# Causal masks of a first score pass: from accumulating matmuls in PSUM to VectorE's add-and-minimum instruction

## The reference

```python
x = x + 0.5 * ffn(layernorm(x))      # 8 experts, I = 512, silu(x G^T) * (x U^T) D^T, top-p routing
x = x + attn(layernorm(x))           # 16 query heads of 16, 4 key/value heads, RMS norm, rope
x = x + 0.5 * ffn(layernorm(x))
# inside attn
attn = jnp.einsum('bhqd,bhkd->bhqk', q * scale, k)
attn = jnp.where(causal[None, None], attn, -jnp.inf)
attn = jax.nn.softmax(attn, axis=-1)
```

## Time and profile before

| | |
|---|---|
| median of 3 runs | 1226.78 us (1225.18 to 1227.13) |
| the profiled execution, its own time | 1226.45 us |
| its span in the profile | 1224.7 us |
| busy PE, DVE, POOL, ACT | 95%, 65%, 55%, 47% |

### The profile page before, as it was taken

The page is one execution under the profiler, slowest core; times in us unless marked ns, Lnnn a source line. Parts: engine busy times, 40 slices in busy tenths (PEclk is TensorE's granted clock), DMA queues, the critical chain, the costliest instruction groups (busy, mean ns, idle before and its releaser), DMA issues.

```text
span 1224.7 us, 22657 instructions
## 1 busy us (share of the span) xinstructions
PE 1165.3 (95%) x8315; PEld 701.2 (57%) x8315; DVE 796.2 (65%) x1571; ACT 578.0 (47%) x954; POOL 669.8 (55%) x740
## 2 busy tenths in 40 slices
PE   4699999998999899999899999899999999999998
PEld 2355555565555566666566566566565565666655
DVE  5688787567866766666766667767567555554444
ACT  3444454343456545555455554554644545333332
POOL 4454334357567766666666677577564546333332
PEclk9799999999999999999999999999999999999999
DMA  6112120000000000000000000000000000000000
GB/s 217 45 56 82 52 65 1 1 1 1 1 1 1 1 1 2 1 1 2 1 2 1 1 1 2 1 18 2 1 2 1 18 1 1 1 10 9 1 1 19
DMA packets 10107, 19.25 MB, mean 16 GB/s; under 512 B 2192, under 2 KB 6800, under 8 KB 10000
## 3 DMA queue, kind: packets, MB, share of 16 engines
q1 hardware_dynamic: 8992, 14.64, 3.7%
q10 hardware_dynamic: 1008, 3.15, 0.7%
HBM read 15.70 MB, written 2.10 MB: 15 GB/s over the span
## 4 chain that ended last, share of the span: by engine, by line
PE 69%; DVE 7%; POOL 3%; issue 2%; ACT 1%; DVEq 0%; ACTq 0%; POOLq 0%
PE YB L297 20%; PE G L278 19%; PE U L278 19%; PE S L420 2%; POOL RR L1067 1%; PE S L446 1%; PE S L461 1%; DVE TS L680 1%; PE S L352 1%; DVE MXN L891 1%; DVE TS L684 1%; ACT TS L509 1%; PE S L392 1%; PE S L396 1%; PE S L398 1%
## 5 line engine op out<-in xcount | busy, mean ns | idle before, releaser
L1011 POOL TENSOR_TENSOR HS<-TS,HS 128x512 f16<-128x512 f32 x256 | 303.1, 1184 | 433.5 <-ACT HS L516 433.1
L680 DVE SCALAR_TENSOR_TENSOR TS<-TS,G 128x512 f32<-128x512 f32 x256 | 175.6, 686 | 372.0 <-ACT TS L509 371.6
L297 PE MATMUL YB<-W,HS 128*128 128x256 f16 x3036 | 374.7, 273 | 20.3 <-DVE X L700 20.3
L278 PE MATMUL G<-XS,W 128*128 128x512 f16 x1536 | 377.5, 382 | 2.9 <-ACT W L523 1.8
L278 PE MATMUL U<-XS,W 128*128 128x512 f16 x1536 | 376.4, 381 | 0.0
L297 PEld LDWEIGHTS YB<-W,HS 128*128 128x128 f16 x3036 | 292.2, 98 | 98.7 <-DVE X L700 29.9
L509 ACT ACTIVATE TS<-G,TSC 128x512 f32<-128x512 f32 x256 | 175.5, 686 | 297.5 <-PE U L278 290.9
L516 ACT ACTIVATE HS<-TS 128x512 f16<-128x512 f32 x256 | 161.2, 630 | 273.8 <-DVE TS L684 268.1
L278 PEld LDWEIGHTS U<-XS,W 128*128 128x128 f16 x1536 | 151.1, 98 | 183.9 <-issue 4.4
L278 PEld LDWEIGHTS G<-XS,W 128*128 128x128 f16 x1536 | 147.6, 98 | 136.4 <-issue 6.4
L684 DVE SCALAR_TENSOR_TENSOR TS<-TS,U 128x512 f32<-128x512 f32 x256 | 175.8, 687 | 8.8
(11 more groups left out here) (160 smaller groups left out, 861.6 us busy)
## 6 DMA issues: line engine op xcount, KB each, us to landing
out_y<-X SPq DMA_DIRECT2D x16, 128.0 KB, 1.7
X<-in_x SPq DMA_DIRECT2D x3, 512.0 KB, 6.1
room<-in_gate SPq DMA_DIRECT2D x3, 512.0 KB, 3.1
room<-in_up SPq DMA_DIRECT2D x3, 512.0 KB, 3.2
room<-in_down SPq DMA_DIRECT2D x3, 512.0 KB, 3.9
QKT<-in_gate SPq DMA_DIRECT2D x3, 512.0 KB, 3.6
QKT<-in_up SPq DMA_DIRECT2D x3, 512.0 KB, 3.7
QKT<-in_down SPq DMA_DIRECT2D x3, 512.0 KB, 4.5
```

The source lines that it names most:

```text
L278: mm = eng.matmul(bank[:, :], W[:, e, wl, jj, kk * I + m * P:kk * I + (m + 1) * P], flat(XS16[:, b % 2, xl, kk, :, :], 'cq'), start=q == 0 ...
L297: mm = eng.matmul(out, HS[:, j % 2, hl, kk, m * P:(m + 1) * P], W[:, e, wl, 2, kk * D:(kk + 1) * D], start=kk + hl + wl == 0, stop=kk == K ...
L680: eng.scalar_tensor_tensor(TS[:, k % 3, :], TS[:, k % 3, :], 1.0, GB[k % 2][:, :], ALU.add, ALU.mult).then_inc(L['v_t'].sem, 1)
L1011: eng.tensor_tensor(HS[:, j % 2, 1, m, :], TS[:, k % 3, :], HS[:, j % 2, 0, m, :], ALU.subtract).then_inc(L['g_lo'].sem, 1)
```

## The change

`pe_max` leaves the mask matmuls out and signals after the last score matmul of each bank. MB becomes two blocks of 128 columns, the first all 0, the second the mask. `dve_max` no longer reduces a bank in one instruction: for each head it issues one `tensor_tensor_reduce`, which computes (scores + mask) x -1, writes it back over the scores in PSUM, and gives the minimum of it. That is 8 instructions of 128 columns in an even pass and 4 of 256 columns in an odd one, instead of 2 of 512 columns. RWR, a small tile used before the first routing, now lies in LG, and `flat` is defined earlier.

```diff
-        RWR = sb('RWR', [P, 2, KD, E], F32)
+        RWR = LG[:, :, :].rearrange('p (a k) e -> p a k e', a=2)
-        MB = sb('MB', [P, P], F16)
+        MB = sb('MB', [P, 2, P], F16)
...
-                        eng.matmul(bank[:, q * P:(q + 1) * P], QT1[rows(h), 2 * kv + q % 2, :], keys[rows(h), 0, kv, :], start=q == 0, stop=False, skip_group_check=True, tile_position=(64 * h, 0))
-                for bank in (S0, S1):
-                    mm = eng.matmul(bank[:, :].rearrange('p (g k) -> p g k', g=G), ident16[:, :], MB[:, :].unsqueeze(1).broadcast_to([P, G, P]), start=False, stop=True, skip_group_check=True)
+                        mm = eng.matmul(bank[:, q * P:(q + 1) * P], QT1[rows(h), 2 * kv + q % 2, :], keys[rows(h), 0, kv, :], start=q == 0, stop=q == 3, skip_group_check=True, tile_position=(64 * h, 0))
+                        if q == 3:
+                            mm.then_inc(L['p_mx'].sem, 1)
...
-                for bank in (S0, S1):
-                    mm = eng.matmul(bank[:, :].rearrange('p (a b) -> p a b', a=2)[:, :, P:2 * P], ident16[:, :], MB[:, :].unsqueeze(1).broadcast_to([P, 2, P]), start=False, stop=True, skip_group_check=True)
-            mm.then_inc(L['p_mx'].sem, 1)
...
+            if n == 0:
+                eng.wait_ge(s_i2, 2)
+            heads, width = (4, P) if t % 2 == 0 else (2, 2 * P)
+            mask = flat(MB[:, :, :], 'ak')[:, 2 * P - width:]
             for h, bank in ((0, S0), (1, S1)):
-                if t % 2 == 0:
-                    x, out = (bank[:, :].rearrange('p (a g k) -> p a g k', a=2, g=2), MXN[:, 2 * j:2 * j + 2, :, h])
-                else:
-                    x, out = (bank[:, :].rearrange('p (g k) -> p g k', g=2), MXN[:, j, :, h])
-                eng.tensor_reduce(out, x, AX.X, ALU.max, negate=True).then_inc(L['v_mp'].sem, 1)
+                for g in range(heads):
+                    out = MXN[:, 2 * j + g // 2, g % 2, h:h + 1] if t % 2 == 0 else MXN[:, j, g, h:h + 1]
+                    x = bank[:, g * width:(g + 1) * width]
+                    mx = eng.tensor_tensor_reduce(x, x, mask, -1.0, 3.0e38, ALU.add, ALU.min, out)
+                mx.then_inc(L['v_mp'].sem, 1)
```

More of the change, by code:

```diff
@@ L115, in sem, with flat @@
             return ctx.enter_context(nc.semaphore(name))
+        def flat(ap, dims):
+            return ap.rearrange(f"p {' '.join(dims)} -> p ({' '.join(dims)})")
         X = sb('X', [P, NT, D], F32)
@@ L395, in pe_max @@
                     for h, bank in ((0, S0), (1, S1)):
-                        eng.matmul(bank[:, q * 2 * P:(q + 1) * 2 * P], QT1[rows(h), 2 * j + q, :], keys[rows(h), :, j, :], start=q == 0, stop=False, skip_group_check=True, tile_position=(64 * h, 0))
-                for bank in (S0, S1):
-                    mm = eng.matmul(bank[:, :].rearrange('p (a b) -> p a b', a=2)[:, :, P:2 * P], ident16[:, :], MB[:, :].unsqueeze(1).broadcast_to([P, 2, P]), start=False, stop=True, skip_group_check=True)
-            mm.then_inc(L['p_mx'].sem, 1)
+                        mm = eng.matmul(bank[:, q * 2 * P:(q + 1) * 2 * P], QT1[rows(h), 2 * j + q, :], keys[rows(h), :, j, :], start=q == 0, stop=q == 1, skip_group_check=True, tile_position=(64 * h, 0))
+                        if q == 1:
+                            mm.then_inc(L['p_mx'].sem, 1)
         def pe_qtp2(eng, t, s):
@@ L555, in act_qc @@
             if t:
-                eng.wait_ge(*L['p_mx'].at(MAXN[t - 1], 'ab'))
+                eng.wait_ge(*L['p_mx'].at(MAXN[t - 1], 'b'))
             eng.wait_ge(*L['p_qt'].at(t, 'q'))
@@ L882, in dve_max @@
             t, j = MAXP[n]
-            eng.wait_ge(*L['p_mx'].at(n, 'ab'))
+            eng.wait_ge(*L['p_mx'].at(n, 'b'))
             if j == 0:
                 eng.wait_ge(*L['v_mm'].at(t - 1, 'm2'))
+            if n == 0:
+                eng.wait_ge(s_i2, 2)
+            heads, width = (4, P) if t % 2 == 0 else (2, 2 * P)
+            mask = flat(MB[:, :, :], 'ak')[:, 2 * P - width:]
             for h, bank in ((0, S0), (1, S1)):
-                if t % 2 == 0:
-                    x, out = (bank[:, :].rearrange('p (a g k) -> p a g k', a=2, g=2), MXN[:, 2 * j:2 * j + 2, :, h])
-                else:
-                    x, out = (bank[:, :].rearrange('p (g k) -> p g k', g=2), MXN[:, j, :, h])
-                eng.tensor_reduce(out, x, AX.X, ALU.max, negate=True).then_inc(L['v_mp'].sem, 1)
+                for g in range(heads):
[3 more added lines that the diff above has]
+                mx.then_inc(L['v_mp'].sem, 1)
         def dve_mm(eng, t):
@@ L1231, in _ @@
             eng.memset(LOW[:, :, :], 1.0).then_inc(s_i1, 1)
-            eng.memset(MB[:, :], 0.0).then_inc(s_i1, 1)
+            eng.memset(MB[:, :, :], 0.0).then_inc(s_i1, 1)
             eng.wait_ge(s_i1, 7)
             eng.affine_select(out=LOW[:, :, :], in_=LOW[:, :, :], compare_op=ALU.is_ge, fill=0.0, base=-1, pattern=[[1, E], [-1, E]], channel_multiplier=0).then_inc(s_i1, 1)
-            eng.affine_select(out=MB[:, :], in_=MB[:, :], compare_op=ALU.is_ge, fill=MASKED, base=0, pattern=[[-1, P]], channel_multiplier=1).then_inc(s_i2, 1)
+            eng.affine_select(out=MB[:, 1, :], in_=MB[:, 1, :], compare_op=ALU.is_ge, fill=MASKED, base=0, pattern=[[-1, P]], channel_multiplier=1).then_inc(s_i2, 1)
             eng.memset(VS[:, :, :, :, :], 1.0).then_inc(s_i2, 1)
```

2 lines of the change are left out of this document (removed), and 2 rows, old and new, of the table L.

## The result

The changed kernel takes **1229.61 us** (median of 20 runs, 1224.23 to 1233.93), the kernel before 1226.13 (20 runs, 1223.71 to 1227.47); the ratio is **1.0026**, 95% interval 1.0015 to 1.0036. It is slower by about 3.5 us, where I forecast 1.5 us faster. The profiled execution took 1229.79 us, its span is 1228.0 (1224.7 before).

The account below looks back on a forecast made before the run. It took TensorE, busy 95% of the span, to bound the kernel, with VectorE holding it in places. Terms 3.2 - 3.0 - 0.7 - 1.0 = -1.5 us took 1226.78 to 1225.3 us, range 1221.0 to 1232.5.

Parts of the forecast that it names:

- the opening: VectorE's queue is full there, so its longer passes delay L700 and TensorE: 0.99 + 4 x 0.56 = +3.2 us.
- three batches without routing: Masks save 1.57 us before a last pass without slack, which loses 0.56: -1.01 each, -3.0 us.
- three with routing: Two odd passes on the VectorE and GpSimd chain lose 1.12, masks ahead save 1.34: -0.22 each, -0.7 us.
- the last batch: Routing but no further projections, so only its last pass is on the path: 1.57 - 0.56, -1.0 us.
- TensorE's saving, 14.4 us: Mask matmuls removed from TensorE: 0.44 us in each of 16 even passes, 0.23 in each of 32 odd ones.
- The pair, 0.307 and 0.441 us: VectorE's price per new instruction pair, 128 or 256 columns; an even pass takes 1.26 us more, an odd one 0.56.
- 0.107: Price in us of each VectorE pair's second, one-column instruction, taken from L907 because it follows a long instruction.
- Rival 1: VectorE's pairs do not overlap, each instruction costing its whole length: +4.8 us, 1231.6; chance 0.27.
- rival 3: Reading and writing PSUM at once takes VectorE two cycles a column: +14.7 us, 1241.5; chance 0.07.
- rival 2: The second instruction of a VectorE pair costs only 0.05 us: -5.0 us, 1221.8; chance 0.24.
- Their cost is 0: Batch passes at a+4, a+6, a+15 and a+22: extra VectorE time is covered by its wait for ACT's tanh.
- The wait for L700 was to grow by 13 us: TensorE's summed wait for VectorE's L700 rises from 20.3 us by about 13 (14.4 saved less 1.5).

Follow-up runs that it names:

- e17: Changed kernel with the maxima's cast and subtraction behind the next L700 only in the three batches without routing; 1221.60 us, ratio 0.9967.
- e1: Kernel before with the mask matmuls left out and the old reductions kept, no mask added in the first pass; 1219.76 us, ratio 0.9956.
- e15: Changed kernel with late cast, a+24 pass behind RMS steps, first routing step ahead of L871, and the opening's six passes as before; 1209.51 us.
- e4: Changed kernel with the maxima's cast and subtraction behind the next L700 in the seven batches' last odd pass; 1213.60 us, ratio 0.9911.
- e13: Changed kernel with the last odd pass of the seven batches as before (masks on TensorE, one reduction per bank); 1219.54 us, ratio 0.9952.
- e18: Changed kernel with the maxima's cast and subtraction behind the next L700 only in the four batches with routing; 1220.37 us, ratio 0.9953.

## Why the prediction was wrong

At the marker the stretch comes apart like this, beside what I had put:

| | put | measured |
|---|---|---|
| the opening | +3.2 | +0.55 |
| three batches without routing | -3.0 | +2.2 |
| three with routing, low clock apart | -0.7 | -1.1 |
| the last batch | -1.0 | -1.4 |
| two stretches of low clock | no term | +3.4 |
| sum | -1.5 | +3.7 |

The runs give the same sum another way: -4.4 us with the three casts out of the way (689.76, e17, against 694.18), +4.7 for the three held casts (1.86 us at the marker less the 0.28 left with the cast late, three times), +3.4 for two stretches of low clock. Two things are behind the wrong sign: the held casts, which bring the change from a gain to nothing, and the clock, which brings it from nothing to a loss.

- **TensorE's saving, 14.4 us.** The price was right (0.41 for an even pass and 0.22 for an odd one at the marker, 0.44 and 0.23 in my text). That all of it counts ahead of the fixed places was not: without any cost on VectorE (e1) a third to a half of it comes out, and in a batch without routing 1.03 us of about 1.7.
- **The pair, 0.307 and 0.441 us.** It is 0.249 and 0.38: the accumulator's read overlaps the next instruction altogether, and my ground for 0.107, that it follows a long instruction, was wrong. Rival 1, pairs that do not overlap, is refuted, and so is rival 3, half rate; the slow-down came by no way that I had listed. By price alone rival 2 was the right one, -5.0 us, and with the three casts out of the way the stretch gives -4.4.
- **The opening, +3.2 us.** It was +0.55, mostly from the lower price; the wait now at 333.92 is 1.01 us, where I put 2.0. That the masks save nothing there held (e15).
- **Batches without routing, -1.01 each.** This is the step that failed: "no slack ... the last pass's 0.23 turns into waiting, and 0.56 is lost". These batches measure +0.71, +0.76 and +0.77. In the first, 1.46 is saved ahead, 0.54 is lost at L420, 0.22 is saved by the last pass's masks, and 1.86 is lost in the wait for L700. I took the cast and the subtraction as 0.2 us each whatever comes ahead, while rows of the same lines were 1.02 and 0.62 us long behind the routings, and did not lay GpSimd's list beside. The margin was 0.24 us, the cast moved by 0.35. Waits of about 0.8 us were forecast, 1.75 came. The 0.54 is a smaller miss: the passes at a+22 and a+24 delay GpSimd's power, and TensorE's L420 behind it starts at 499.60 for 499.08.
- **Batches with routing, -0.22 each.** The first gives +0.75, since its even passes and their saving end in a wait for L700 of 0.83 us at 366.95; the second and third -0.9 each without their low clock. The last batch gave -1.43 where I put -1.0. "Their cost is 0" for the even passes held in all other batches: the whole 0.81 is kept.
- **The clock** had no term, and cost 3.4 us in the profiled execution; its mean clock, 0.990, or a lower one stands in 12 of the 20 runs. It is tied to the new waits by the runs that take waits away (e4, e13, e17, e18), not explained by them.
- The wait for L700 was to grow by 13 us and grew by 7.9; another 1.6 us are at L420 behind the routings, where TensorE stood 0.44 to 0.49 us before and 0.97 to 1.08 now, for L799.

The range held the result, the sign did not, and that the range held was partly luck: the errors went both ways, with pairs too dear by 3.5 us or more, and casts and clock, 8.1 us, left out.

## What to carry over

Where VectorE and GpSimd run side by side, look at every short cast, copy or two-source instruction between the work that grows and the instruction that another engine waits for: if the same line has two durations in the trace (0.20 and 1.02 us here), look for another engine's instruction that runs at the same time; here a shift of a third of a microsecond decided. Put such an instruction behind the one that is waited for, or use a form that is not held, as the reduction was here; the order was worth more (6 us in the kernel before, 14 in the changed one, 3.4 of it the clock) than the change itself, 4 to 5 us. A saving on the busiest engine is worth only what the next in line lets through: a run with the work simply left out (e1: a third to a half of 14.4 us) shows it.

## What had not been expected of the hardware

A reduction of sixteen columns takes 0.23 us beside GpSimd's instruction, a cast of the same columns 1.11. The second instruction of an add-and-minimum pair, 139 ns long, starts together with the next one and adds nothing to the queue that the rows show. An add-and-minimum that reads and writes PSUM and reads a mask in SBUF goes at a column a nanosecond, 0.25 us for 128 and 0.38 for 256 columns, with no sign of half rate, and the 128-column pairs kept their 0.25 us while GpSimd ran its low half beside them:

```profile
300.80 1.16 POOL L1015 TENSOR_TENSOR HS<-TS,HS 128x512 f16<-128x512 f32 x1
300.91 0.33 DVE L894 CUSTOM_DVE_ANT_0 S<-S,MB 128x128 f32<-128x128 f32 x1
301.16 0.33 DVE L894 CUSTOM_DVE_ANT_0 S<-S,MB 128x128 f32<-128x128 f32 x1
```

The granted clock of TensorE fell to its lower level for 3.4 us behind some waits of 2.04 us and not behind others of 2.93.
